# An attention and mixture-of-experts kernel on one core: a quad's rows sent from an earlier slot, and a table made ahead of a copy

## Time and profile before

| | |
|---|---|
| median of 3 runs | 706.51 us (705.89 to 706.66) |
| the profiled execution | 707.03 us |
| its span, first to last instruction | 705.3 us |
| mean granted TensorE clock | 0.702 of full speed |
| TensorE busy | 417.5 us, 59% |
| VectorE busy | 580.2 us, 82% |
| ScalarE busy | 539.3 us, 76% |
| GpSimd busy | 459.0 us, 65% |

### The profile page before, as it was taken

The page is one execution under the profiler, slowest core; times in us unless marked ns, Lnnn a source line. Parts: engine busy times, 40 slices in busy tenths (PEclk is TensorE's granted clock), DMA queues, the critical chain, the costliest instruction groups (busy, mean ns, idle before and its releaser), DMA issues.

```text
span 705.3 us, 14439 instructions
## 1 busy us (share of the span) xinstructions
PE 417.5 (59%) x3943; PEld 281.5 (40%) x3943; DVE 580.2 (82%) x1487; ACT 539.3 (76%) x896; POOL 459.0 (65%) x538
## 2 busy tenths in 40 slices
PE   0259554545365464564644642238878999999454
PEld 0024232324233243242432421226656767777343
DVE  2688668787999989989899899867958998888756
ACT  0035258999989989999899997636668899999763
POOL 9355144273474888978888868557777877777700
PEclk9999765555555555555555555558999999999768
DMA  8559999979920031210310010127656766663098
GB/s 175 73 101 264 319 318 322 289 212 276 301 70 7 12 96 39 73 39 22 85 44 5 33 34 22 43 60 138 154 107 148 138 141 123 151 128 91 1 343 316
DMA packets 149615, 93.66 MB, mean 133 GB/s; under 512 B 77123, under 2 KB 143644, under 8 KB 149539
## 3 DMA queue, kind: packets, MB, share of 16 engines
q1 hardware_dynamic: 139266, 75.04, 42.8%
q0 software_dynamic: 10272, 17.70, 7.7%
HBM read 23.61 MB, written 61.24 MB: 120 GB/s over the span
## 4 chain that ended last, share of the span: by engine, by line
ACT 30%; PE 19%; DVE 18%; issue 15%; POOL 8%; SPq 5%; DMA 3%; POOLq 0%; DVEq 0%; ACTq 0%
POOL expert_rows L743 5%; PE pS L1842 5%; PE pX L1858 4%; PE pP L1842 3%; ACT S_sq L950 3%; ACT L950 2%; ACT S_u L845 2%; ACT S_sq L945 2%; ACT S_sq L922 2%; PE pX L1616 2%; ACT S_g L895 2%; ACT pTs L927 2%; DVE S_e L1399 2%; SPq L532 2%; ACT arena L839 2%
## 5 line engine op out<-in xcount | busy, mean ns | idle before, releaser
L743 POOL DMA_INDIRECT expert_rows<-stage,dest x118 | 124.5, 1055 | 37.5 <-issue 31.1
L677 POOL DMA_INDIRECT region<-rows,slots x60 | 67.8, 1130 | 16.3 <-issue 15.1
L1858 PE MATMUL pX<-w2s,stage 128*128 x472 | 59.1, 253 | 12.5 <-ACT stage L980 9.9
L592 POOL TENSOR_TENSOR w1s<-stage,w1s 128x384 f16<-128x384 f32 (+8 forms) x72 | 60.9, 846 | 7.0 <-ACT w1s L811 1.7
L1616 PE MATMUL pX<-arena,WA 128*128 128x384 f16 x86 | 34.4, 502 | 39.0 <-ACT arena L839 29.4
L1736 PE MATMUL pP<-idb,S_p 128*88 128x128 bf16 x192 | 25.8, 315 | 53.1 <-DVE S_p L1356 53.1
L677 POOL DMA_INDIRECT region<-arena,slots x36 | 43.5, 1209 | 13.2 <-issue 8.4
L1858 PEld LDWEIGHTS pX<-w2s,stage 128*128 128x128 f16 x472 | 39.6, 99 | 28.5 <-issue 25.7
L713 POOL CAST oq<-o 128x384 bf16<-128x384 int8 x24 | 23.0, 957 | 39.1 <-ACT o L905 39.1
L1761 PE MATMUL pP<-WpT,oq 128*128 128x192 bf16 x72 | 14.8, 339 | 56.7 <-ACT pTs L930 56.7
L665 POOL CAST arena<-arena 128x384 bf16<-128x384 int8 x42 | 29.3, 710 | 27.0 <-ACT arena L839 26.8
(11 more groups left out here) (437 smaller groups left out, 1665.0 us busy)
## 6 DMA issues: line engine op xcount, KB each, us to landing
region<-zrow SPq DMA_DIRECT2D x45, 800.0 KB
w1s<-expert_rows SPq DMA_DIRECT2D x16, 384.0 KB, 7.7
stage<-in_L_ffn_w_dram SPq DMA_DIRECT2D x24, 192.0 KB
stage<-in_L_ffn_w_dram SPq DMA_DIRECT2D x8, 384.0 KB
w2s<-expert_rows SPq DMA_DIRECT2D x8, 384.0 KB, 11.8
arena<-in_x_dram SPq DMA_DIRECT2D x4, 672.0 KB
expert_rows<-stage,dest POOLq DMA_INDIRECT x118
out_dram<-xsel SPq DMA_DIRECT2D x8, 198.0 KB
```

The source lines that it names most:

```text
L592: pool.tensor_tensor(ws[rows, min(kind + 1, 3), two, to:to + width], st[rows, :, at:at + width], ws[rows, kind, two, to:to + width], ALU.s ...
L677: pool.indirect_dma_start(region_rows, bass.IndirectOffsetOnAxis(ap=slots[q % 3][:, i, m:m + 1], axis=0), rows[q % 3][:, i, :].bitcast(I16 ...
L743: pool.indirect_dma_start(y_dram, bass.IndirectOffsetOnAxis(ap=dest[(st - 7) % 8][:, j:j + 1], axis=0), ysb[b][:, j, :], None, bounds_chec ...
L1858: ins = pe.matmul(y_ps[:, j, :], lhs, w2s[:, kind, bass.ds(k_, 1), :].rearrange("p o f -> p (o f)"), start=n == 0, stop=n == 4)
```

## The change

It has two parts.

First, SEND becomes 8: a quad's twelve sends are due in the slot that finds their places (i = 2), one slot earlier. The room of the slots i = 0, 1, 2 becomes 3, 4, 5 where it was 3, 3, 6. GpSimd's slot i = 2 no longer places sends at its front nor round the casts of v: all five come at its end, behind `low_x`. By the list, slots 8+3q, 9+3q and 10+3q then hold 5, 3 and 4 sends of quad q, where slots 9+3q to 11+3q held 3, 3 and 6. At the end, slot 23 holds 5 (of quad 5; before 6, of quad 4), slot 24 holds 5 as before, slot 25 holds 2 for 7, and slot 26 holds quad 6's 12 as before.

Second, in slot 25 (NT + 1) VectorE's `step_table(0)` is moved from the end of the slot to the place ahead of `evac_rT(..., 0)`, and TensorE's `spread_table(0)` from the second half of its slot to its first instruction.

```diff
-        COEFFS, NORM, TURN, GATE, RANK, SEND = 5, 6, 7, 7, 8, 9
+        COEFFS, NORM, TURN, GATE, RANK, SEND = 5, 6, 7, 7, 8, 8
...
-            room = 5 if st == NT else len(queue) if st > NT else (3, 3, 6)[st % 3]
+            room = 5 if st == NT else len(queue) if st > NT else (3, 4, 5)[st % 3]
...
                 if st <= NT:
-                    send((3, 0, 3)[i] if st < NT else 2)
+                    send((3, 0, 0)[i] if st < NT else 2)
...
                     if i == 2:
-                        send(1)
                         cast_v(q + 1, rn, 0, fill(st, "v", 0))
                         cast_v(q + 1, rn, 1, fill(st, "v", 1))
-                        send(1)
                 if i == 2 and st // 3 + 2 < NQ:
                     low_x(q + 2)
                 send(len(pending))
...
+                if st == NT + 1:
+                    step_table(0)
                 if quad_at(st, TURN) is not None:
                     evac_rT(quad_at(st, TURN), 0)
...
                 if st == NT:
                     step_blocks(0)
-                if st == NT + 1:
-                    step_table(0)
...
             def slot(st, n, q):
                 i, nxt = st % 3, st // 3 + 1 < NQ
+                if st == NT + 1:
+                    spread_table(0)
...
                 if st == NT:
                     count_rows(0)
-                if st == NT + 1:
-                    spread_table(0)
```

## The result

The changed kernel took 718.07 us (median of 4 runs, 716.26 to 718.74) against 706.2 us for the kernel before on the same chip (4 runs): a ratio of 1.015, 95% interval 1.0119 to 1.0181, so 8.4 to 12.8 us slower. The forecast was 718.9. The profiled execution of the changed kernel took 716.26 us, its lowest run, with a span of 714.5.

The account below looks back on a forecast made before the run. Taken as bound: a chain changing between ScalarE, TensorE and VectorE, with GpSimd off it by 2.17 us of cover. Terms 7.35 + 2.1 + 2.7 + 0.3 + 0 = 12.4 us gave 719.4 profiled, forecast 718.9; range 710 to 728.

Parts of the forecast that it names:

- The mechanism: Slots: eight sends behind low_x delay low_pair and low_rows, so TensorE's turning and VectorE's copy wait; quads 48 to 49 us.
- The terms of a quad: Quads from 226, 272, 318 us: sends 5.84, less 0.56 idle, 0.66 cast and 2.17 cover, leave 2.45 us each.
- the lower bound of 0.97: Shortest send in the trace, 0.97 us, taken as lower bound for an added send: 5.08 us for four, 1.7 a quad.
- The cover: Time from the end of low_rows, 294.64, to TensorE's turning of those rows, 296.81: 2.17 us, 2.2 in each of three quads.
- The first quad: Quad from 226 us: counted like the next two, four sends added to four before low_pair, 2.45 us lost.
- The fourth and fifth quads: Quad from 364 us: +2.1 us past a cover of 4.23; slots 20 to 22: +2.7 us, no cover.
- The experts' start: After the slots: SyncE's first load 3 to 4 us sooner, expert part unchanged; term 0, lower end -0.5 us.
- Rival 1: Faster: earlier first loads of SyncE decide, giving 1 to 3 us if GpSimd's delay stays covered; about 704.5; chance 0.09.
- Rival 2: Much slower: every added send meets VectorE's short passes at 1.85 us; 729 to 736 us; chance 0.12.
- the trace agrees in kind: Port rule for GpSimd sends beside VectorE's two-port passes: said to match the trace, 1.85 us beside such passes, 0.97 elsewhere.

Follow-up runs that it names:

- e3: The changed kernel with six of low_pair's twelve subtractions on 8 columns only, sends as changed: 706.52 us, ratio 0.9988 to the kernel before.
- e4: The kernel before, without the change, with six of low_pair's twelve subtractions on 8 columns only: 702.59 us, ratio 0.9942.
- e8: The kernel before with low_rows placed behind the sixth of low_pair's twelve subtractions instead of behind the twelfth, on a slower chip: 805.08 us, ratio 1.0053.
- e10: e8 run again, on a third chip, beside a trace of the kernel before: 799.49 us, ratio 1.0055.
- e9: The kernel before, unchanged, run on the third chip for its trace there: 794.25 us, ratio 1.0001.
- e11: Both parts of the change, with low_rows inside low_pair behind its sixth piece, against the kernel before, on the third chip: 802.37 us, ratio 1.0081.

## Why the prediction was right

**The mechanism.** Each step of it stands in the trace after: the sends in a row, the unmoved start behind low_x, low_pair later, the turning released by line 334 in five quads, VectorE idle ahead of the copy. That idle time came to 15.4 us over all copies, 3.9 the longest, for 5.4 before.

**The terms of a quad.** From the end of low_x to low_pair: forecast +4.62 us, measured 11.06 for 7.50, +3.56. Four more sends took 5.25 us, not 5.84: those added stood at 0.98 to 1.08 us, near the lower bound of 0.97, where I took 1.16. The cast fell to 0.52, 0.44 below the 0.96 that I took. The block low_pair plus low_rows, which I had left at 14.44, took 15.09: +0.65. These three misses nearly cancel: low_rows ends 4.2 us later in place of 4.62, and 4.2 - 2.17 = 2.0 is the 2.02 of the table. The cover, the one number on which the sign hangs, was right, and e3 beside e4 shows that it decides in the first four quads. That the size came out within a microsecond is in part luck.

**The first quad was counted wrong.** The prediction put four sends between low_x and low_pair in all three quads alike. In the one that begins at 226 us there are three in the kernel before, since nothing is due ahead of slot 9, and so the change adds five. They took 6.5 us more than the three. The cover there is 2.22 us, the rows' low parts end 4.49 us later counted from low_x, and 2.27 us is left, which is the 2.30 of the table: 0.79 us of idle time before the cast, a cast 0.63 us shorter and 14.04 us for 14.53 in low_pair and low_rows made up for the fifth send.

**The fourth and fifth quads** came to 1.56 for 2.1 and 2.43 for 2.7. The fourth is as the ones before it: shorter sends, and 15.10 us for 14.47 in the block. In the fifth the sends were not short. Two of the eight took 1.62 and 2.02 us, and they began 0.8 us behind the slots that they waited for. They held low_pair until 427.65 us (GpSimd in order of time):

```profile
426.96 0.72 POOL L713 CAST oq<-o 128x384 bf16<-128x384 int8 x1
427.65 6.32 POOL L592 TENSOR_TENSOR w1s<-stage,w1s 128x384 f16<-128x384 f32 x6
```

Counted from the copy before it, low_pair began 3.7 us later, not 2.7, and the block then took 14.13 us for 15.41. That these two misses cancel is luck as well.

**The experts' start.** The loads did come sooner. SyncE's queue in the changed kernel, its first load:

```profile
476.92 1.35 SPq L522 DMA_TRANSPOSE S_g<-region  x1
```

And VectorE, where quad 6's places are found:

```profile
483.20 0.17 DVE L1277 TENSOR_TENSOR slots<-arena,bad 128x12 int32<-128x12 f32 x1
```

The load lies 6.3 us ahead, for 1.0 before (473.23 and 474.23), so 5.3 us sooner where I had said 3 to 4. I had put that down to the sends; with the sends alone (e1) the load lies only 2.2 us ahead, with the table alone (e2) 1.0, so it took both. And it is worth nothing: from the slots of quad 6 to the end it is 231.3 us for 231.1. Rival 1 fell with this. (Its bound of 2.73 us for four sends leaves out the 0.66 us of the shorter cast that the sum counts; four at their shortest pass 3.39 as well.) That the stage gains nothing because its first work hangs on VectorE's norms is the prediction's reading; no run tested it.

**Rival 2** (every added send at 1.85 us) fell: from the second to the fourth quad none of the four added ones took over 1.08 us beside VectorE's passes, in the fifth two came near that price, and the sends taken from the front of slot 2, where three had taken 5.56 us, got shorter. The two groups of sends by form (busy us, mean ns | idle before) average 1088 and 1096 ns for 1130 and 1209:

```profile
L677 POOL DMA_INDIRECT region<-rows,slots x60 | 65.3, 1088 | 22.5 <-issue 16.2 <-DVE rows L1279 6.3
L677 POOL DMA_INDIRECT region<-arena,slots x36 | 39.5, 1096 | 19.0 <-issue 9.6 <-DVE arena L1279 9.5
```

So the change does save GpSimd 6.5 us of sends, and 2.4 of casts, and loses because they were saved where GpSimd had time to spare. Beside these rows: the rule of the Trainium skill (SBUF — State Buffer, "Who interferes with whom") that a VectorE copy, cast or tensor_scalar in its two-port mode and GpSimd's DMA issue shut each other out, applied to every added send, would have made the whole 735.7 us. No such price stands at the place where most of the sends went: the send at 281.64, beside VectorE's tensor_scalar of line 1226, took 0.98 us. The prediction's sentence that the trace agrees in kind was also too strong. Of the three sends at slot 14's front, the one at 305.67 took 1.95 us beside scalar_tensor_tensor and tensor_tensor passes alone.

**What I had wrong beside the forecast.** I expected e4 to give almost nothing, and it gives 4.1 us. After e4 I took the end of low_rows for what the kernel before loses there; e8 and e10 bring that end forward by some 7 us and gain nothing. What e4 gains lies, in the fifth quad at least, in VectorE's passes, which are shorter beside shorter subtractions. I had looked at GpSimd only as something that releases others late, and not as something that lengthens VectorE's work beside it. No version that was run beats the kernel before with its full work.

## What to carry to other kernels

Before work is moved on an engine that is "off the chain", find the one instruction on it that a busy engine waits for, and count the time between its end and its use (here 2.17 us). Up to this cover an insertion ahead of it is free; well beyond it each microsecond was paid here in every round, however much the engine saved elsewhere. Shortening a neighbour of the moved work (here the subtractions of low_pair) tests this, if it is done on both kernels: on its own it also changes how long the other engine's passes take beside it, and only the difference of the two (e3 and e4) tells what the move costs.

## What the runs showed of the hardware

- The same kernel took 706 us on one chip and 795 and 800 on two others. Over the quads the traces agree within 2 us (229.2 and 231.1), but in the experts' steps the one of e9 moved less data in the same time. Busy time of PE, PEld, DVE, ACT and POOL, clock, DMA share and GB/s from 510 to 640 us, the kernel before on the first chip:

```profile
510.00:640.00 130.00, 122.24 (x1106) 91.62 (x1104) 109.60 (x301) 112.83 (x268) 100.93 (x96) 0.99 0.66 136
```

  The same stretch of e9:

```profile
510.00:640.00 130.00, 95.48 (x740) 68.46 (x740) 77.85 (x234) 74.05 (x170) 70.54 (x69) 0.85 0.44 96
```

  VectorE there waits 34.3 us (480 to 700 us) for something that the profile gives only as "remote". The cause was not looked into.
- An indirect send of GpSimd took 0.96 to 1.02 us, with 0.30 us between two, in 65 of 96 cases before and 69 of 96 after, and up to 2.04 us in others. Eight in a row were no slower one by one than four: the fifth to eighth at 278.98 to 282.92 took 0.98 to 1.08 us.
- VectorE's S_w took 1.31 to 1.35 us beside a send of GpSimd or beside nothing, in all of 182 cases, and 1.39, 1.87 or 3.38 us beside its subtractions (e9, e10, e11); esum took 0.47 or 0.86 (e9 and e10). In e10 the quads came out 1.9 us longer although low_rows ended some 7 us sooner in the quad; that such half microseconds are what did it is read from the traces.
